# One copy instead of two for the projected rows of a graph attention layer, and a finish that adds the node's own row in two halves

## The chip, the cores and the metric

The kernel runs on one core of a Trainium2 chip. The metric is the device time of one execution in microseconds (us), as the median of several runs. Engines are TensorE (PE), VectorE (DVE), ScalarE (ACT), GpSimd (POOL) and the queues that issue DMAs (SP and POOL here).

## The reference

3125 nodes with 1024 features, 50000 edges sorted by target. A graph attention layer with 4 heads of 256 columns comes first and two graph layers with mean aggregation follow; each part has a residual.

```python
h = jnp.maximum(_layernorm(x), 0.0)
xp = (h @ W).reshape(N, H, C)                  # the projected rows
a_src = einsum('nhc,hc->nh', xp, att_src); a_dst = einsum('nhc,hc->nh', xp, att_dst)
e = leaky_relu(a_src[src] + a_dst[dst], 0.2)   # every node also has an edge to itself
alpha = softmax of e over the edges of each dst
out = segment_sum(xp[src] * alpha[:, :, None], dst)
x = x + relu(out + bias)
h = jnp.maximum(_layernorm(x), 0.0)
h1 = relu(h @ W_self0 + mean(h) @ W_neigh0 + b0)
x = x + (h1 @ W_self1 + mean(h1) @ W_neigh1 + b1)
```

## The kernel before

The nodes are cut into 25 tiles of 125 rows. Precision near float32 comes from pairs of float16 numbers: a high half and a low half that holds what the high one lost. A matrix product then takes three products of halves. The kernel runs in stages, one after the other, and between two stages all engines meet.

`normalize_x` (about 135 to 275 us) normalizes the input and projects the first 4 tiles beside it. `edge_scores` (to about 639 us) projects the other 21 tiles, in pieces between the small matmuls that fetch the scores of the edges, and turns the scores into weights. Both write each projected tile twice to DRAM. ACT takes the float32 sums out of PSUM into `rows` (L655, L1131) and copies them to float16 as the high half (L659, L1135). The low half is a subtraction, on DVE in the first stage (L705) and on POOL in the second (L1089). The POOL queue stores `rows` to `xp_rows` (L619, L1087) and the two halves to `xs_rows` (L621, L1091). `rows` is a single buffer: before ACT fills it again it waits for `xp_stored`, the store of the tile before, and in `edge_scores` also for `rows_lo`.

`aggregate` (to about 1333 us) gathers rows of `xs_rows` by the edges and sums them by target, weighted, into `acc`, which stays in SBUF. A node's edge to itself isn't in the list of edges.

`gat_finish` (1333 to 1657 us) adds that edge and does the rest of the layer. Its engines run over the tiles m side by side:

- SP loads x and `xp_rows` of tile m (L1621, L1622) into two slots each, once `x1_ready` says that tile m - 2 has been used, and stores the product of an older tile (L1627). After the loads of tile 1 it issues the load of 4 MB of split weights and that of b0, before the loads of tile 2.
- DVE does `values(m)`: 4 `scalar_tensor_tensor` instructions, one a head (L1682), for own row times own weight plus `acc`; 4 more (L1687) for the division and the bias; one for relu and residual (L1690); then the statistics (L1693 to L1697). Then `normalize(m)`: after ACT's square root, L1705 and L1706, the shift. Then `finish(m - 2)` (L1724), which takes the product of tile m - 2 out of PSUM, once `prod_done` is given. Between tiles 1 and 2 stands `bound` (L1714 to L1717 and three more).
- ACT writes the normalized row as float32 and as the high half (L1756, twice), and moves turned halves out of PSUM (L1742).
- POOL makes the low half (L1649, one `tensor_tensor`) and gives `lo_done`.
- PE works in the order: 16 of the 48 matmuls of tile n (L1787), the 16 transposes of tile n + 1 (L1775), which wait for `lo_done`, then the other 32 matmuls of tile n (L1791), after which it gives `prod_done`.

DVE's order within a tile and PE's are written out by hand and can't change with the times. Two aggregations, the second layer's products and the last product follow, to the end at 3406 us.

Of the kernel before, what the change touches and what calls it, by code (L numbers as in the profile page):

```python
# [11 lines left out]
def bass_gat_sage_sage(nc, x_in, src_in, dst_in, w_gat, att_src, att_dst, gat_bias,  # L12
# [63 lines left out]
    def scratch(name, shape, dt=f32):  # L76
        return nc.dram_tensor(name, shape, dt).ap()
# [2 lines left out]
    hn_rows = scratch("hn_rows", (N, 2 * D), f16)  # L80


    xp_rows = scratch("xp_rows", (N, D))
    xs_rows = scratch("xs_rows", (N, 2 * D), f16)
    slot_rows = scratch("slot_rows", (2, NS * CH), bf16)
    x1_rows = scratch("x1_rows", (N, D))
# [86 lines left out]
    with top:  # L173
# [354 lines left out]
        def normalize_x(w16, att_n, early_in):  # L528
            with ExitStack() as ctx:
# [26 lines left out]
                hn_ready, lo_done = sem("hn_ready"), sem("lo_done")  # L556
                turned, hi_moved, lo_moved, att_done, read_out = sem("turned"), sem("hi_moved"), sem("lo_moved"), sem("att_done"), sem("read_out")
                prod_done, rows_out, rows_hi, rows_lo = sem("prod_done"), sem("rows_out"), sem("rows_hi"), sem("rows_lo")
                xp_stored, xs_stored = sem("xp_stored"), sem("xs_stored")
                v_stats, v_norm = sem("v_stats"), sem("v_norm")  # L560
                block = ctx.enter_context(nc.Block())
                STEPS = NT + 2
# [49 lines left out]
                @block.gpsimd  # L612
                def _(g):
                    load_pieces = piece_loader(g, early_in)
                    for r in range(PIECE_BUFS):
                        load_pieces(r)
                    for p in range(FIRST):
                        g.wait_ge(rows_out, p + 1)
                        g.dma_start(tiles(xp_rows)[:, p:p + 1, :], rows[:, :].unsqueeze(1)).then_inc(xp_stored, 16)  # L619
                        g.wait_ge(rows_lo, p + 1)  # L620
                        g.dma_start(tiles(xs_rows)[:, p:p + 1, :], parts16[:, :].unsqueeze(1)).then_inc(xs_stored, 16)  # L621
                    g.wait_ge(xp_stored, 16 * FIRST)
                    g.wait_ge(xs_stored, 16 * FIRST)

                @block.scalar
                def _(a):
                    a.wait_ge(cleared, 1)
                    for s in range(STEPS):
                        if s < NT:
                            slot = s % 2  # L630
                            a.wait_ge(var_ready, s + 1)
                            a.activation(rstd[:, slot:slot + 1], mv[:, slot, 1:2], ACT.Sqrt).then_inc(std_ready, 1)
                            a.wait_ge(norm_ready, s + 1)
                            if s >= 2:
                                a.wait_ge(lo_done, s - 1)
                                a.wait_ge(turned, s - 1)
                                if stores_before(s):
                                    a.wait_ge(stored[slot], CUT * stores_before(s))
                            for dst in (hn[:, slot, :], a16[0:TN, slot, 0:D]):
                                last = a.activation(dst, x_sb[:, s % XS, :], ACT.Relu, bias=shift[:, slot:slot + 1],  # L640
                                                    scale=rstd[:, slot:slot + 1])
                            last.then_inc(hn_ready, 1)
                        if 2 <= s:
                            n = s - 2
                            a.wait_ge(turned, n + 1)
                            if n >= FIRST + 2:
                                a.wait_ge(att_done, n - 1)
                            a.activation(home(n)[:, 0], turn_ps[n % 2][:, 0], ACT.Copy).then_inc(hi_moved, 1)
                        piece = piece_of(s - 1)
                        if piece is not None and piece[1] == PIECES - 1:  # L650
                            p = piece[0]
                            a.wait_ge(prod_done, p + 1)
                            if p > 0:
                                a.wait_ge(xp_stored, 16 * p)
                            a.activation(rows[:, :], out_ps[0:TN, :], ACT.Copy, scale=1.0 / (UP * D)).then_inc(rows_out, 1)  # L655
                            a.wait_ge(rows_out, p + 1)
                            if p > 0:
                                a.wait_ge(xs_stored, 16 * p)
                            a.activation(parts16[:, 0:D], rows[:, :], ACT.Copy).then_inc(rows_hi, 1)  # L659
# [298 lines left out]
        def edge_scores(key_r, mask_r, att_n, w16, weight_e, high_e, early_in):  # L958


            with ExitStack() as ctx:
# [52 lines left out]
                now_ready = sem("now_ready")  # L1014
                spread, taken, kept = sem("spread"), sem("taken"), sem("kept")
                row_turned, row_moved, prod_done = sem("row_turned"), sem("row_moved"), sem("prod_done")
                rows_out, rows_hi, rows_lo, xp_stored, xs_stored = sem("rows_out"), sem("rows_hi"), sem("rows_lo"), sem("xp_stored"), sem("xs_stored")
                w_in = [sem(f"w_in{i}") for i in range(WBUF)]
                w_stored = [sem(f"w_stored{i}") for i in range(WBUF)]
                w_hi, w_lo, w_reduced, w_scaled = sem("w_hi"), sem("w_lo"), sem("w_reduced"), sem("w_scaled")  # L1020
# [60 lines left out]
                def _(g):  # L1081
                    load_pieces = piece_loader(g, early_in)

                    def low(p):
                        n = FIRST + p
                        g.wait_ge(rows_out, p + 1)
                        g.dma_start(tiles(xp_rows)[:, n:n + 1, :], rows[:, :].unsqueeze(1)).then_inc(xp_stored, 16)  # L1087
                        g.wait_ge(rows_hi, p + 1)
                        g.tensor_tensor(parts16[:, D:2 * D], rows[:, :], parts16[:, 0:D], ALU.subtract).then_inc(rows_lo, 1)  # L1089
                        g.wait_ge(rows_lo, p + 1)  # L1090
                        g.dma_start(tiles(xs_rows)[:, n:n + 1, :], parts16[:, :].unsqueeze(1)).then_inc(xs_stored, 16)  # L1091
# [10 lines left out]
                            low(p)  # L1102
                    for p in range(LEFT - AFTER, LEFT):
                        low(p)
                    g.wait_ge(xp_stored, 16 * LEFT)
                    g.wait_ge(xs_stored, 16 * LEFT)

                @block.scalar
                def _(a):
# [16 lines left out]
                    def evacuate(p):  # L1126
                        a.wait_ge(prod_done, p + 1)
                        if p > 0:
                            a.wait_ge(xp_stored, 16 * p)
                            a.wait_ge(rows_lo, p)  # L1130
                        a.activation(rows[:, :], out_ps[0:TN, :], ACT.Copy, scale=1.0 / (UP * D)).then_inc(rows_out, 1)  # L1131
                        a.wait_ge(rows_out, p + 1)
# [442 lines left out]
        def gat_finish(acc, acc_x, mem):  # L1575
            with ExitStack() as ctx:
                sb, ps, sem = opener(ctx, "fin")
                carve = carver(mem)
                x_sb = sb("x_sb", [TN, 2, D])
                xp_sb = carve([TN, 2, D])  # L1580
                a_t = [carve([P, 2, KT, P], f16) for _ in range(2)]
                b0_sb = carve([P, D])
                bias_sb = sb("bias_sb", [P, D])
# [32 lines left out]
                def _(sp):  # L1616
                    def load(m):
                        if m >= 2:
                            sp.wait_ge(x1_ready, m - 1)
                        for a, b in CUTS:  # L1620
                            sp.dma_start(x_sb[a:b, m % 2, :], x_in[m * TN + a:m * TN + b, :]).then_inc(x_loaded[m % 2], 16)  # L1621
                            sp.dma_start(xp_sb[a:b, m % 2, :], xp_rows[m * TN + a:m * TN + b, :]).then_inc(x_loaded[m % 2], 16)  # L1622

                    def store(n):
                        sp.wait_ge(read_out, n + 1)
# [31 lines left out]
                def _(v):  # L1657
# [11 lines left out]
                    v.wait_ge(bias_in, 16)  # L1669

                    def values(m):
                        PER = 2 + 1 + 3
                        slot = m % 2
                        step = chain(v, v_val, PER * m)
                        v.wait_ge(x_loaded[slot], 2 * CUT * (m // 2 + 1))
# [3 lines left out]

                        for h in range(H):  # L1680
                            cols = slice(h * C, (h + 1) * C)
                            last = v.scalar_tensor_tensor(val[:, slot, cols], xp_sb[:, slot, cols], own_n[:, m, h:h + 1],  # L1682
                                                          acc[:, m, cols], ALU.mult, ALU.add)
                        step(last)
                        for h in range(H):
                            cols = slice(h * C, (h + 1) * C)
# [364 lines left out]
```

## Time and profile before

| | |
|---|---|
| median of 3 runs | 3411.33 us (3408.95 to 3415.5) |
| profiled execution | 3407.41 us |
| its span, first to last instruction | 3405.8 us |
| mean granted clock of PE | 0.962 |
| PE busy | 2971.0 us, 87% |
| DVE busy | 2373.0 us, 70% |
| ACT busy | 1205.5 us, 35% |
| POOL busy | 1637.1 us, 48% |
| DMA | 934.91 MB, mean 275 GB/s |

Busy shares are means over stages with different limits. What an edit is worth has to be read in its own stage, from the waits of the engines there.

### The profile page before, as it was taken

How to read it: one execution, taken by the hardware profiler on the slowest of the kernel's cores; microseconds unless marked ns; L12 is line 12 of the kernel's file. 1: busy time of each engine (PE TensorE's matmuls, PEld its weight loads, DVE VectorE, ACT ScalarE, POOL GpSimd, SP SyncE). 2: the span in 40 equal slices, each digit the busy share in tenths (PEclk: the TensorE clock that was granted, in tenths of full speed). 3: DMA queues.
4: the chain of work that ended last, by engine and by line, in shares of the span. 5: the costliest groups of instructions: out<-in, count | busy, mean ns of one | idle time of the engine just before them, and what ended most of it. 6: DMA issues, size and time to landing. Idle time of an engine off the chain costs nothing. (4 is left out here: it accounts for less than half of the span.)

```text
span 3405.8 us, 66706 instructions
## 1 busy us (share of the span) xinstructions
PE 2971.0 (87%) x20462; PEld 1711.8 (50%) x20462; DVE 2373.0 (70%) x3944; ACT 1205.5 (35%) x2639; POOL 1637.1 (48%) x1592
## 2 busy tenths in 40 slices
PE   0477998399999996999799999998799999997998
PEld 0245665188888885444244444443344444443444
DVE  9687998699999998888466666664455555554333
ACT  3454443288888886444112222222000000001111
POOL 5102332267777774222466666662566666662000
PEclk9978999699999998999899999999899999998999
DMA  2797995388888888777699999995999999996444
GB/s 79 226 292 226 353 344 171 110 295 311 307 316 307 307 309 292 217 220 226 247 354 330 331 338 328 331 338 211 321 346 328 329 328 333 315 331 241 133 138 120
DMA packets 282530, 934.91 MB, mean 275 GB/s; under 512 B 53795, under 2 KB 54799, under 8 KB 282368
## 3 DMA queue, kind: packets, MB, share of 16 engines
q0 software_dynamic: 217792, 713.64, 59.9%
q1 hardware_dynamic: 64576, 219.26, 20.6%
q8 instruction: 83, 1.36, 0.2%
q14 instruction: 79, 0.65, 0.1%
HBM read 879.78 MB, written 130.57 MB: 297 GB/s over the span
## 5 line engine op out<-in xcount | busy, mean ns | idle before, releaser
L1522 PE MATMUL gagg_sum_ps<-gagg_got,gagg_hot_hi 128*128 128x256 f16 x3520 | 591.4, 273 | 92.8 <-ACT gagg_hot_hi L1493 58.8
L1493 ACT ACTIVATE gagg_hot_hi<-gagg_hot,all_mem 128x128 f16<-128x128 f16 x1760 | 538.0, 388 | 165.6 <-DVE gagg_hot L1433 165.4
L1410 POOL DMA_INDIRECT gagg_got<-xs_rows,all_idx x440 | 503.8, 1145 | 191.9 <-issue 131.4
L1410 POOL DMA_INDIRECT agg_got<-h_rows,all_idx x440 | 435.3, 989 | 317.8 <-PE agg_sum_ps L1538 175.9
L1838 POOL DMA_INDIRECT agg_got<-h_rows,all_idx x440 | 437.6, 994 | 268.2 <-PE agg_sum_ps L1991 145.7
L1458 DVE TENSOR_TENSOR sums_acc<-agg_sum_ps,sums_acc 125x1024 f32 x220 | 269.5, 1225 | 320.3 <-PE agg_sum_ps L1538 317.1
L1522 PE MATMUL gagg_sum_ps<-gagg_got,gagg_hot_lo 128*128 128x256 f16 x1760 | 481.5, 274 | 0.0
L1903 DVE TENSOR_TENSOR sums_acc<-agg_sum_ps,sums_acc 125x1024 f32 x220 | 268.9, 1222 | 246.9 <-PE agg_sum_ps L1991 245.0
L1991 PE MATMUL agg_sum_ps<-agg_got,all_mem 128*128 128x512 f16 x1760 | 415.4, 383 | 24.2 <-DVE all_mem L1872 16.7
L1538 PE MATMUL agg_sum_ps<-agg_got,agg_hot 128*128 128x512 f16 x1760 | 418.1, 381 | 17.1 <-DMA agg_got<-h_rows,all_idx 12.4
L1522 PEld LDWEIGHTS gagg_sum_ps<-gagg_got,gagg_hot_hi 128*128 128x128 f16 x3520 | 329.3, 98 | 136.3 <-ACT gagg_hot_hi L1493 68.2
L1439 DVE TENSOR_TENSOR gagg_hot_lo<-gagg_hot,all_mem 128x512 f16<-128x512 f16 x440 | 284.7, 689 | 9.3
L1991 PEld LDWEIGHTS agg_sum_ps<-agg_got,all_mem 128*128 128x128 bf16 x1760 | 170.7, 98 | 235.8 <-issue 29.9
L1976 PE MATMUL agg_out_ps<-agg_w,all_mem 128*128 128x512 f16 x1200 | 283.6, 381 | 2.0 <-ACT all_mem L1933 2.0
L1538 PEld LDWEIGHTS agg_sum_ps<-agg_got,agg_hot 128*128 128x128 bf16 x1760 | 167.4, 98 | 232.2 <-issue 36.6
L951 PE MATMUL agg_out_ps<-agg_w,all_mem 128*128 128x512 f16 x1200 | 283.5, 379 | 0.0
L1458 DVE TENSOR_TENSOR sums_acc<-gagg_sum_ps,sums_acc 125x1033 f32 x220 | 270.7, 1230 | 13.9 <-PE gagg_sum_ps L1527 12.0
L864 PE MATMUL neigh_out_ps<-neigh_w,neigh_a_t 128*128 128x512 f16 x1200 | 264.4, 381 | 4.7 <-DMA neigh_w<-split_w 4.7
L930 ACT ACTIVATE all_mem<-agg_turn_ps 128x2048 f16<-128x2048 f16 x25 | 46.9, 1877 | 601.2 <-PE agg_turn_ps L938 601.2
L1320 PE MATMUL edg_out_ps<-gatw_w,edg_a_t 128*128 128x512 f16 x1008 | 238.2, 381 | 5.3 <-ACT edg_rows L1131 5.3
L1925 ACT ACTIVATE all_mem<-sums_acc,all_deg_inv 125x1024 f16 x25 | 28.7, 1148 | 465.8 <-issue 402.1
L1976 PEld LDWEIGHTS agg_out_ps<-agg_w,all_mem 128*128 128x128 f16 x1200 | 117.6, 98 | 144.9 <-issue 2.4
(290 smaller groups left out, 4013.1 us busy)
## 6 DMA issues: line engine op xcount, KB each, us to landing
gatw_piece<-slot_rows POOLq DMA_DIRECT2D x56, 512.0 KB
split_w<-edg_w_out SPq DMA_DIRECT2D x32, 512.0 KB, 8.2
agg_got<-h_rows,all_idx POOLq DMA_INDIRECT x880, 7.0
x_rows<-fin_val POOLq DMA_DIRECT2D x25, 500.0 KB
h_rows<-fin_h POOLq DMA_DIRECT2D x25, 500.0 KB
out_dram<-neigh_rows POOLq DMA_DIRECT2D x25, 500.0 KB
norm_x_sb<-in_x_dram SPq DMA_DIRECT2D x25, 448.0 KB
fin_x_sb<-in_x_dram SPq DMA_DIRECT2D x25, 448.0 KB
```

The lines of the kernel that those rows point to most:

```text
L864: last = t.matmul(o, l, r, start=start, stop=stop)
L951: last = t.matmul(o, l, r, start=first, stop=final)
L1410: g.indirect_dma_start(out=got[:, k % R, :], out_offset=None, in_=rows_in[:, :], in_offset=bass.IndirectOffsetOnAxis(ap=idx[:, k:k + 1], a ...
L1439: v.tensor_tensor(hot_lo[:, u % HOTS, :, :], hot[:, u % HOTS:u % HOTS + 1, :].to_broadcast([P, H, P]), weight_e[:, ds(s, 1), 1, 0:H].rearr ...
L1458: v.tensor_tensor(acc[:, tl, 0:WIDE], sum_ps[n % 2][0:TN, 0:WIDE].rearrange("p (a d) -> p a d", a=1), acc[:, tl, 0:WIDE], ALU.add).then_in ...
L1493: last = a.activation(hot_hi[:, u % HOTS, h, :], hot[:, u % HOTS, :], ACT.Copy, scale=high_e[:, ds(s, 1), h])
L1522: t.matmul(sum_ps[n % 2][:, h * C:(h + 1) * C], hot_k[:, u % HOTS, h, :], got[:, u % R, part * D + h * C:part * D + (h + 1) * C], start=(u ...
L1538: last = t.matmul(sum_ps[n % 2][:, q * HALF:(q + 1) * HALF], hot[:, u % HOTS, :], got[:, u % R, cols], start=(u == steps[0] and part == 0) ...
L1838: g.indirect_dma_start(out=got[:, k % R, :], out_offset=None, in_=rows_in[:, :], in_offset=bass.IndirectOffsetOnAxis(ap=idx[:, k:k + 1], a ...
L1903: v.tensor_tensor(acc[:, ds(tile, 1), 0:D], sum_ps[g % 2][0:TN, :].rearrange("p (a d) -> p a d", a=1), acc[:, ds(tile, 1), 0:D], ALU.add). ...
L1976: last = t.matmul(o, l, r, start=start, stop=stop)
L1991: last = t.matmul(sum_ps[g % 2][:, q * HALF:(q + 1) * HALF], hot[:, u % R, :], got[:, u % R, cols], start=(u % PAIR == 0 and part == 0), s ...
```

## The change

The float32 copy is gone. `xs_rows`, the pair of halves, is the only copy. Its size per row is that of `xp_rows` (2048 float16 numbers instead of 1024 float32 ones, 4 KB each), so the finish loads as many bytes as before, in as many DMAs, into a tile of the same size. The finish adds the own row in two passes of 4 instructions: low half times weight plus `acc`, then high half times weight plus that result, with a semaphore step of its own between them. Where ACT waited for the float32 store before it refilled `rows`, it now waits for the low half's subtraction.

```diff
-    xp_rows = scratch("xp_rows", (N, D))
     xs_rows = scratch("xs_rows", (N, 2 * D), f16)
...
                     for p in range(FIRST):
                         g.wait_ge(rows_out, p + 1)
-                        g.dma_start(tiles(xp_rows)[:, p:p + 1, :], rows[:, :].unsqueeze(1)).then_inc(xp_stored, 16)
                         g.wait_ge(rows_lo, p + 1)
                         g.dma_start(tiles(xs_rows)[:, p:p + 1, :], parts16[:, :].unsqueeze(1)).then_inc(xs_stored, 16)
-                    g.wait_ge(xp_stored, 16 * FIRST)
...
                             if p > 0:
-                                a.wait_ge(xp_stored, 16 * p)
+                                a.wait_ge(rows_lo, p)
...
                     def low(p):
                         n = FIRST + p
                         g.wait_ge(rows_out, p + 1)
-                        g.dma_start(tiles(xp_rows)[:, n:n + 1, :], rows[:, :].unsqueeze(1)).then_inc(xp_stored, 16)
                         g.wait_ge(rows_hi, p + 1)
...
-                    g.wait_ge(xp_stored, 16 * LEFT)
...
                         if p > 0:
-                            a.wait_ge(xp_stored, 16 * p)
                             a.wait_ge(rows_lo, p)
...
-                xp_sb = carve([TN, 2, D])
+                xs_sb = carve([TN, 2, 2 * D], f16)
...
-                            sp.dma_start(xp_sb[a:b, m % 2, :], xp_rows[m * TN + a:m * TN + b, :]).then_inc(x_loaded[m % 2], 16)
+                            sp.dma_start(xs_sb[a:b, m % 2, :], xs_rows[m * TN + a:m * TN + b, :]).then_inc(x_loaded[m % 2], 16)
...
-                        PER = 2 + 1 + 3
+                        PER = 3 + 1 + 3
...
                         for h in range(H):
                             cols = slice(h * C, (h + 1) * C)
-                            last = v.scalar_tensor_tensor(val[:, slot, cols], xp_sb[:, slot, cols], own_n[:, m, h:h + 1],
+                            last = v.scalar_tensor_tensor(val[:, slot, cols], xs_sb[:, slot, D + h * C:D + (h + 1) * C], own_n[:, m, h:h + 1],
                                                           acc[:, m, cols], ALU.mult, ALU.add)
+                        step(last)
+                        for h in range(H):
+                            cols = slice(h * C, (h + 1) * C)
+                            last = v.scalar_tensor_tensor(val[:, slot, cols], xs_sb[:, slot, cols], own_n[:, m, h:h + 1],
+                                                          val[:, slot, cols], ALU.mult, ALU.add)
                         step(last)
```

## Rows read from the trace of the kernel before

**Rows 1.** Busy time by stretch: start:end, length, each engine, granted clock, DMA share

```profile
core 0: us, PE busy (x) PEld busy (x) DVE busy (x) ACT busy (x) POOL busy (x), PEclk, DMA share, GB/s
350.00:400.00 50.00, 48.88 (x548) 30.90 (x546) 49.25 (x78) 24.11 (x63) 16.88 (x21) 1.00 0.98 352
...
1354.00:1651.00 297.00, 287.02 (x1599) 139.50 (x1600) 226.44 (x385) 131.45 (x121) 79.89 (x74) 0.98 0.69 212
```

**Rows 2.** Timeline, DVE in one tile of the finish: start, duration, operation, [idle]

```profile
1453.56 0.21 DVE L1706 TENSOR_SCALAR fin_shift<-fin_mv,fin_rstd 125x1 f32<-125x1 f32 x1
...
1455.09 1.28 DVE L1724 SCALAR_TENSOR_TENSOR fin_rows<-fin_out_ps,fin_post,all_mem 125x1024 f32<-125x1024 f32 x1 [1.31 <-PE fin_out_ps L1791]
1456.29 3.63 DVE L1682 SCALAR_TENSOR_TENSOR fin_val<-all_mem,fin_own_n,sums_acc 125x256 f32<-125x256 f32 x4
1459.95 1.67 DVE L1687 SCALAR_TENSOR_TENSOR fin_val<-fin_val,fin_z,fin_bias_sb 125x256 f32<-125x256 f32 x4
...
1465.38 0.21 DVE L1706 TENSOR_SCALAR fin_shift<-fin_mv,fin_rstd 125x1 f32<-125x1 f32 x1
1466.51 1.28 DVE L1724 SCALAR_TENSOR_TENSOR fin_rows<-fin_out_ps,fin_post,all_mem 125x1024 f32<-125x1024 f32 x1 [0.92 <-PE fin_out_ps L1791]
```

**Rows 3.** Timeline, GpSimd and TensorE in the same tile and in an earlier one

```profile
1389.47 1.06 PE L1775 MATMUL fin_turn_ps<-all_ident,fin_h 128*128 128x128 f16 x16
...
1400.72 1.06 PE L1775 MATMUL fin_turn_ps<-all_ident,fin_h 128*128 128x128 f16 x16
...
1456.32 2.12 POOL L1649 TENSOR_TENSOR fin_h<-fin_h_sb,fin_h 125x1024 f16<-125x1024 f32 x1 [4.38 <-ACT fin_h L1756]
1458.50 1.07 PE L1775 MATMUL fin_turn_ps<-all_ident,fin_h 128*128 128x128 f16 x16
1459.40 7.07 PE L1791 MATMUL fin_out_ps<-fin_w,all_mem 128*128 128x512 f16 x32
...
1468.13 2.43 POOL L1649 TENSOR_TENSOR fin_h<-fin_h_sb,fin_h 125x1024 f16<-125x1024 f32 x1 [4.37 <-ACT fin_h L1756]
```

**Rows 4.** Timeline, DVE at the start of the finish, and its last tile

```profile
1360.76 1.22 DVE L1714 TENSOR_REDUCE fin_largest<-all_mem 128x1 f32<-128x1024 f32 x1 [1.87 <-DMA all_mem<-in_L_gnn_b_dram]
...
1365.80 1.68 DVE L1682 SCALAR_TENSOR_TENSOR fin_val<-all_mem,fin_own_n,sums_acc 125x256 f32<-125x256 f32 x4 [1.29 <-DMA all_mem<-xp_rows]
...
1372.94 0.21 DVE L1706 TENSOR_SCALAR fin_shift<-fin_mv,fin_rstd 125x1 f32<-125x1 f32 x1
1373.31 1.28 DVE L1724 SCALAR_TENSOR_TENSOR fin_rows<-fin_out_ps,fin_post,all_mem 125x1024 f32<-125x1024 f32 x1
...
1383.38 0.21 DVE L1706 TENSOR_SCALAR fin_shift<-fin_mv,fin_rstd 125x1 f32<-125x1 f32 x1
1386.22 1.28 DVE L1724 SCALAR_TENSOR_TENSOR fin_rows<-fin_out_ps,fin_post,all_mem 125x1024 f32<-125x1024 f32 x1 [2.63 <-PE fin_out_ps L1791]
...
1395.21 0.21 DVE L1706 TENSOR_SCALAR fin_shift<-fin_mv,fin_rstd 125x1 f32<-125x1 f32 x1
...
1628.08 0.21 DVE L1706 TENSOR_SCALAR fin_shift<-fin_mv,fin_rstd 125x1 f32<-125x1 f32 x1
```

**Rows 5.** Groups by line, whole kernel: busy and mean, then idle before

```profile
L1211 DVE SCALAR_TENSOR_TENSOR edg_w_out<-edg_w_buf,all_w_up,edg_w_out 128x1024 f16<-128x1024 f32 x32 | 44.6, 1394 | 1.9 <-ACT edg_w_out L1142 1.9
L1690 DVE SCALAR_TENSOR_TENSOR fin_val<-fin_val,fin_x_sb 125x1024 f32<-125x1024 f32 x25 | 30.6, 1225 | 0.9
```

**Rows 6.** Who waited for whom, 300 to 560 us: us, times, longest

```profile
ACT edg_w_out L1142 <- DMA edg_w_buf<-in_L_gnn_W_neigh_dram: 7.2, 3, 3.3
DVE edg_mask L1189 <- DMA gatw_piece<-slot_rows: 3.6, 1, 3.6
ACT edg_w_out L1142 <- DMA edg_w_buf<-in_L_gnn_W_self_dram: 2.9, 2, 1.6
```

**Rows 7.** Busy time by stretch, two stretches with gaps on TensorE

```profile
140.00:160.00 20.00, 15.74 (x175) 9.29 (x173) 18.18 (x33) 11.56 (x14) 0.00 (x0) 0.74 0.87 262
1374.00:1384.00 10.00, 7.68 (x48) 3.84 (x47) 8.84 (x16) 4.96 (x6) 3.51 (x3) 1.00 0.80 235
```

## The prediction on record

> **What bounds the kernel now.** I read first the busy time by stretch, for the stages that the diff touches, then the timeline of the finish tile by tile, then the waits of `edge_scores`.
>
> In the finish PE looks like the bound: busy 287.02 of 297 us [rows 1]. Two transposes without a wait between them stand 11.25 us apart, 1389.47 and 1400.72 [rows 3], and this is PE's own work for one tile. But the shifts (L1706) of tiles 4 and 24 stand at 1395.21 and 1628.08 [rows 4], 20 tiles apart, which is 11.64 us a tile. So PE isn't quite the bound. The timeline shows what is: a ring through all engines that takes two tiles for one turn. From the shift of one tile (1453.56) it is 2.76 us to POOL's subtraction (1456.32); 2.18 to the transposes (1458.50); 8.01 to DVE's L1724 (1466.51), since 32 matmuls of 7.1 us end just before; 1.20 from there to the next L1682 (as 1455.09 to 1456.29); and 9.09 from L1682 to the shift after it (1456.29 to 1465.38) [rows 2, 3]. The sum is 23.24 us for two tiles, 11.62 for one, beside 11.64 measured. That is the check that the ring is the bound, with DVE's `values` as one of its legs.
>
> DVE's own order is shorter. L1724 can follow the shift after 0.37 us (1372.94 to 1373.31 [rows 4]), so it needs 0.37 + 1.20 + 9.09 = 10.66 us a tile; the rest, about 1 us, is its wait for PE, 1.31 and 0.92 us in the two tiles shown [rows 2].
>
> The 9.09 us hold a stall. Four instructions of L1682 take 1.68 us alone [rows 4], but 3.63 us when POOL's subtraction starts 0.03 us after them [rows 2, 3]: 1.95 us lost, nearly POOL's 2.12. So while POOL's subtraction runs, L1682 stands still. A new instruction of this kind can be held up in the same way, but the hold lasts only as long as POOL's one instruction, so the second pass moves it and adds no second one.
>
> **The change part by part.**
>
> New work on DVE: 4 instructions a tile, in a leg of the ring. The low pass is L1682 with another first operand. The trace has no such instruction with a float16 operand beside float32 ones on 256 columns, so I bound it. L1211 mixes both types, on 1024 columns, and takes 1394 ns in the mean; L1690, all float32 on 1024 columns, takes 1225 [rows 5]. So float16 buys nothing there. I take the price of L1682: 1.68 us for four and 0.03 us to the next pass (1456.29 + 3.63 to 1459.95 [rows 2]), 1.71 us a tile. The lower bound is two columns in the time of one: L1690's 1225 ns for 1024 columns and 420 for 256 give 1.05 ns a column, so half the columns of four instructions would save 4 x 128 x 1.05 = 0.54 us and leave 1.2. The upper bound is the price stretched as L1211 is against L1690, 1394/1225, 1.9.
>
> The Trainium skill (VectorE: DVE Perf Modes, the section on the TRN2 errata) prices such an instruction at 58 cycles and its columns, 327 ns for 256 at 0.96 GHz. The row has 1.68 us for four, 420 ns each [rows 4], so the trace does not agree, and by the page's figure the new pass would be an estimated 1.3 us and the whole sum some 5 us smaller.
>
> The ring's new length: 23.24 + 1.71 = 24.95 for two tiles, 12.47 a tile. One more effect: with DVE's wait nearly gone, L1682 starts about 0.9 us before POOL's subtraction, not beside it. When DVE is ahead, POOL waits for the instruction under way and takes 2.43 instead of 2.12 us (1468.13 [rows 3]). With all of these 0.31 us it is 12.63. I take 12.55, 0.91 over 11.64. DVE alone would need 10.66 + 1.71 = 12.37, and PE 11.25: both are shorter, so the ring stays the bound. Twenty tiles (4 to 24) give 20 x 0.91 = 18.2 us.
>
> The start is walked by the shifts [rows 4]. Two tiles of `values` come before `bound`: 3.4 us of new work. `bound` waits 1.87 us for b0, and L1682 of tile 2 waits 1.29 us for its load. Both loads are queued behind the 4 MB of weights, and I leave them where they are. The two waits take up 3.16 of the 3.4. But POOL's subtraction of tile 1, 3.4 us later too, now reaches into L1682 of tile 2 (1.68, so not held, before) and costs about 0.7. So the shift of tile 2 comes 0.3 + 1.7 + 0.7 = 2.7 us late, at 1375.6. Tile 3 follows on DVE alone, + 1.7: 4.4 late, at 1387.8. Tile 4 is held by the ring: 1375.6 + 2.76 + 2.5 + 8.01 = 1388.9 for L1724, + 1.20 + 9.09 + 1.71 - 0.1 = 1400.8 for its shift, 5.6 late (the wait of 2.63 us before L1724 at 1386.22 is what shrinks). The last tiles are PE's and hide nothing, for `values(24)` is the last that the transposes wait for. The finish: 5.6 + 18.2 = 23.8 us longer.
>
> Removed in `edge_scores` and `normalize_x`: 25 stores of 500 KB and their issue, about 0.5 us of POOL each. In `edge_scores` the DMA engines are 98% busy at 352 GB/s while PE is busy 48.88 of 50 us [rows 1]. If DMA set the pace, 16 stores between 300 and 560 us would be worth 16 x 1.45 = 23 us. The waits for DMA there sum to 13.7 us [rows 6], 10.1 of them ACT's for weights that are only split beside the main work, and PE has few gaps. I take 0.5 us, between 0 and 6. POOL's issue stood before its wait for ACT's high half and was hidden by that. The wait that takes the place of `xp_stored`, `rows_lo`, was there already in `edge_scores`, and `normalize_x` evacuates four tiles in its 140 us, so the subtraction is long done when ACT asks for it. The last tile's `xs_rows` store, which ends the stage, is issued after POOL's subtraction, not after the other store.
>
> The loads of the finish keep their count, bytes and queue. SP issues the load for tile m + 2 when `x1_ready` comes, 1.71 us later in its tile; it has nearly two tiles to land. Nothing else waits for it. ACT and POOL shift with the ring.
>
> Sum against the profiled execution: 3407.4 + 23.8 - 0.5 = 3430.7 us. It lies 3.9 under the median of the runs (3411.3), so the same difference of 23.3 on the median is 3434.6, and I predict 3435.
>
> **The rivals.** (a) The ring gives way and DVE's order alone sets the pace, because some leg through POOL or PE is shorter than read: 12.37 - 11.64 = 0.73 a tile, 14.6 + 5.6 = 20: 3431. The sum of the legs speaks against it.
> (b) A cheap float16 pass, 1.2 us: the ring 23.24 + 1.2 + 0.3 = 24.74, 12.37 a tile, 0.73 over before, 14.6 and about 3.5 at the start: 3429. L1211 against L1690 speaks against it [rows 5].
> (c) Nothing is shared between tiles and each pays the full pass: 25 x 1.71 = 43: 3454. The ring's turn of two tiles speaks against it, and so do the two DMA waits at the start.
> (d) The clock. PE's gaps grow from 0.4 to 1.3 us a tile. In 140 to 160 us, with PE busy 15.74 of 20, the granted clock is 0.74 [rows 7], so in part 1.2 GHz instead of 2.4. At 0.8 PE's tile would be 11.25/0.8 = 14.1 us, 2.4 over 11.64, 20 times: with the start 3466. Against it: in 1374 to 1384, with a gap of 2.3 us and PE busy 7.68 of 10, the clock is 1.00 [rows 7].
> (e) Faster: `edge_scores` runs at the pace of its DMAs, and stores away are time back. It decides from 24 us, and 25 stores of 1.45 us are worth 36; all of them would have to sit on the path, 3411 - 12 = 3399. PE's 98% there and 13.7 us of waits cap it well below.
> (f) No change to be told from none, 3411: DVE's work hidden in its wait. Its wait is about 1 us and the pass 1.7, so only if (b) and (e) come together.
>
> **How the numbers follow.** The ring 0.64, (a) 0.12, (b) 0.10, (c) 0.04, (d) 0.04, (e) 0.03, (f) 0.03. The predicted time is the ring's. Its own range is 3430 to 3440: 12.47 to 12.63 a tile is 3 us, the relief in `edge_scores` and the runs' spread the rest. The range of 8 in 10 takes in (a) and (b), with up to 6 us of relief, and upwards half the way to (c): 3423 to 3446. A measurement of this kernel tells 0.2%, 7 us, from no change. Faster is (e), 0.03; same is (f), 0.03; slower is the rest, 0.94.
>
> **What the profile after would show.** Two groups of 100 instructions where L1682 was, each about 1.7 us for four when not held, and one hold a tile of 1.9 us, in the first pass. Shifts 12.5 to 12.6 us apart. DVE's wait for PE before L1724 down from about 1 us to 0.3. PE's wait for POOL before the transposes in every tile, about 1.3 us, clock 1.00. The finish 24 us longer and `edge_scores` as long as before within 2 us. I am wrong if shifts stand 12.4 apart without a wait of DVE (a), if the new pass is short (b), if the clock falls in the finish (d), or if `edge_scores` ends much earlier (e).

## The result, and the profile after

The kernel before took 3410.69 us as the median of 6 runs (3406.05 to 3415.5), the changed kernel 3426.09 us (3421.82 to 3430.14). The ratio is 1.0041, with a 95% interval of 1.0028 to 1.0054: slower by 9.6 to 18.4 us. Predicted were 3435 and a range of 3423 to 3446. The sign and the mechanism in the finish hold; the size of the whole came out a third smaller. The profiled executions differ alike, 3421.82 against 3407.41 us.

The head of the page of the kernel after, and what its DMAs moved:

```profile
span 3420.2 us, 66804 instructions
PE 2971.5 (87%) x20462; PEld 1710.8 (50%) x20462; DVE 2424.2 (71%) x4044; ACT 1205.2 (35%) x2639; POOL 1613.6 (47%) x1567
...
DMA packets 278931, 922.11 MB, mean 270 GB/s; under 512 B 53320, under 2 KB 54324, under 8 KB 278768
```

DVE does 51 us more, PE as much as before, and the DMAs move 12.8 MB less (934.91 before), which is the 25 stores. A DVE that is busy 51 us longer, its stalls included, in a kernel 15 us slower says that much of it found room or was paid for elsewhere.

**One tile of the finish.** The DVE timeline of the kernel after; L1676 is the new low pass, L1681 the high pass, L1705 the shift, L1723 the finish of an older tile:

```profile
1426.65 0.21 DVE L1705 TENSOR_SCALAR fin_shift<-fin_mv,fin_rstd 125x1 f32<-125x1 f32 x1
1427.27 1.28 DVE L1723 SCALAR_TENSOR_TENSOR fin_rows<-fin_out_ps,fin_post,all_mem 125x1024 f32<-125x1024 f32 x1 [0.40 <-PE fin_out_ps L1790]
1428.47 3.53 DVE L1676 SCALAR_TENSOR_TENSOR fin_val<-all_mem,fin_own_n,sums_acc 125x256 f32<-125x256 f16 x4
1432.03 1.67 DVE L1681 SCALAR_TENSOR_TENSOR fin_val<-all_mem,fin_own_n,fin_val 125x256 f32<-125x256 f16 x4
1433.74 1.67 DVE L1686 SCALAR_TENSOR_TENSOR fin_val<-fin_val,fin_z,fin_bias_sb 125x256 f32<-125x256 f32 x4
...
1439.17 0.21 DVE L1705 TENSOR_SCALAR fin_shift<-fin_mv,fin_rstd 125x1 f32<-125x1 f32 x1
1439.79 1.28 DVE L1723 SCALAR_TENSOR_TENSOR fin_rows<-fin_out_ps,fin_post,all_mem 125x1024 f32<-125x1024 f32 x1 [0.40 <-PE fin_out_ps L1790]
1440.99 1.27 DVE L1676 SCALAR_TENSOR_TENSOR fin_val<-all_mem,fin_own_n,sums_acc 125x256 f32<-125x256 f16 x3
```

POOL and PE in the same tile:

```profile
1429.41 2.31 POOL L1643 TENSOR_TENSOR fin_h<-fin_h_sb,fin_h 125x1024 f16<-125x1024 f32 x1 [4.38 <-ACT fin_h L1755]
1431.77 1.07 PE L1774 MATMUL fin_turn_ps<-all_ident,fin_h 128*128 128x128 f16 x16 [1.09 <-POOL fin_h L1643]
1432.68 7.07 PE L1790 MATMUL fin_out_ps<-fin_w,all_mem 128*128 128x512 f16 x32
```

Walk the ring. From the shift at 1426.65 it is 2.76 us to POOL, 2.36 to the transposes, 8.02 to DVE's L1723 at 1439.79, 1.20 to the next L1676, and 10.70 from an L1676 to its shift (1428.47 to 1439.17). That is 25.04 us, 12.52 a tile, and the shifts stand 12.52 apart. Against [rows 2, 3] one leg grew by 1.61 (the new pass) and one by 0.18 (POOL waits for the DVE instruction under way). PE now waits 1.09 us for POOL in each tile, where before it waited 0.3 or 0.7 us in about half of them; DVE's wait for PE, mostly between 0.92 and 1.72 us before, has shrunk to 0.40. The first pass is held while POOL runs: 3.53 instead of 1.67. The second, with the same float16 operand, takes 1.67.

**The start and the end of the finish**, DVE after, beside [rows 4]:

```profile
1330.64 1.67 DVE L1676 SCALAR_TENSOR_TENSOR fin_val<-all_mem,fin_own_n,sums_acc 125x256 f32<-125x256 f16 x4 [3.48 <-DMA fin_bias_sb<-in_L_gnn_bias_dram]
...
1350.93 1.22 DVE L1713 TENSOR_REDUCE fin_largest<-all_mem 128x1 f32<-128x1024 f32 x1 [0.15 <-DVE fin_shift L1705]
1352.18 0.16 DVE L1714 TENSOR_TENSOR fin_spread<-all_w_down 128x1 f32<-128x1 f32 x1
...
1354.72 2.19 DVE L1676 SCALAR_TENSOR_TENSOR fin_val<-all_mem,fin_own_n,sums_acc 125x256 f32<-125x256 f16 x4 [1.43 <-DMA all_mem<-xs_rows]
...
1364.09 0.21 DVE L1705 TENSOR_SCALAR fin_shift<-fin_mv,fin_rstd 125x1 f32<-125x1 f32 x1
...
1376.23 0.21 DVE L1705 TENSOR_SCALAR fin_shift<-fin_mv,fin_rstd 125x1 f32<-125x1 f32 x1
...
1389.27 0.21 DVE L1705 TENSOR_SCALAR fin_shift<-fin_mv,fin_rstd 125x1 f32<-125x1 f32 x1
...
1639.49 0.21 DVE L1705 TENSOR_SCALAR fin_shift<-fin_mv,fin_rstd 125x1 f32<-125x1 f32 x1
```

The last two are the shifts of tiles 4 and 24: 250.22/20 = 12.51 us a tile.

**The stages.** I took the first and last start of the instructions that open and close each stage. In us; `pause` runs from the last evacuation of `edge_scores` to the first matmul of the weighted aggregation, `finish` from the first L1682 or L1676 to the last L1724 or L1723:

| | before | after | difference |
|---|---|---|---|
| first edge matrix, start | 281.9 | 280.5 | -1.4 |
| `edge_scores` | 338.6 | 337.2 | -1.4 |
| pause | 30.1 | 28.4 | -1.7 |
| weighted aggregation | 679.2 | 673.0 | -6.2 |
| to the first own row | 12.4 | 11.5 | -0.9 |
| finish | 309.4 | 332.2 | +22.8 |
| first mean aggregation | 680.7 | 680.5 | -0.2 |
| second mean aggregation | 686.8 | 690.8 | +4.0 |
| the other stretches | | | -0.6 |

So the finish lost 22.8 us, as the ring says, and everything before it gave back 11.6, where I had 0.5; what follows the finish took 3.2 back. (The second mean aggregation has the same code in all kernels. In two profiles of the kernel before it took 686.8 and 692.6 us, so 4 us is within its scatter.)

### The profile page after: what moved, and what is told of

Same layout as the page of the kernel before. It is cut to its first block and busy times, and to the rows that moved or that the text cites. A ratio compares the mean times of both kernels' runs of the same rounds, so it can differ in the third digit from the quotient of the medians.

```text
span 3420.2 us, 66804 instructions
## 1 busy us (share of the span) xinstructions
PE 2971.5 (87%) x20462; PEld 1710.8 (50%) x20462; DVE 2424.2 (71%) x4044; ACT 1205.2 (35%) x2639; POOL 1613.6 (47%) x1567
## 5 line engine op out<-in xcount | busy, mean ns | idle before, releaser
L1404 POOL DMA_INDIRECT gagg_got<-xs_rows,all_idx x440 | 491.0, 1116 | 196.4 <-issue 138.5
L1990 PE MATMUL agg_sum_ps<-agg_got,all_mem 128*128 128x512 f16 x1760 | 415.3, 383 | 24.1 <-DVE all_mem L1871 16.7
L1452 DVE TENSOR_TENSOR sums_acc<-gagg_sum_ps,sums_acc 125x1033 f32 x220 | 270.8, 1231 | 11.6 <-PE gagg_sum_ps L1521 9.0
```

Source lines behind the costliest of these rows:

```text
L1404: g.indirect_dma_start(out=got[:, k % R, :], out_offset=None, in_=rows_in[:, :], in_offset=bass.IndirectOffsetOnAxis(ap=idx[:, k:k + 1], a ...
L1452: v.tensor_tensor(acc[:, tl, 0:WIDE], sum_ps[n % 2][0:TN, 0:WIDE].rearrange("p (a d) -> p a d", a=1), acc[:, tl, 0:WIDE], ALU.add).then_in ...
L1990: last = t.matmul(sum_ps[g % 2][:, q * HALF:(q + 1) * HALF], hot[:, u % R, :], got[:, u % R, cols], start=(u % PAIR == 0 and part == 0), s ...
```

## The experiments

They ran on at least three chips, of two speeds. `thin`, `before_again`, `reorder` and `dve_low` ran on a chip of speed A, as did, by its times, the pair above; there the kernel before takes 3410.7 to 3414.6 us. The others ran on two chips of speed B, where it takes 3535.5 and 3536.6. Each ratio is against the kernel before on the same chip; where a difference of whole kernels is given in us, it is of the medians.

### The two halves of the change, alone

`fin_only` is the kernel before with the finish of the kernel after: all stores, and the two passes (the last two parts of the change's diff). `after_again` is the kernel after once more, on this chip.

> Both stores are kept, with their waits and the place of every tensor in DRAM; only the finish is changed (it loads the halves and adds them in two passes). If the finish costs what the ring of two tiles says, it is 22 to 24 us longer than before's and the whole kernel is 22 to 24 us slower than before, 7 us slower than the full change. If the whole is only 15 us slower, the finish is cheaper in the time of the runs than in the one profile, and the stores give nothing back.

`stores_only` is the kernel after with one pass, so it leaves out the low half of the node's own row:

```diff
                         for h in range(H):
                             cols = slice(h * C, (h + 1) * C)
-                            last = v.scalar_tensor_tensor(val[:, slot, cols], xs_sb[:, slot, D + h * C:D + (h + 1) * C], own_n[:, m, h:h + 1],
-                                                          acc[:, m, cols], ALU.mult, ALU.add)
-                        step(last)
...
                             last = v.scalar_tensor_tensor(val[:, slot, cols], xs_sb[:, slot, cols], own_n[:, m, h:h + 1],
-                                                          val[:, slot, cols], ALU.mult, ALU.add)
+                                                          acc[:, m, cols], ALU.mult, ALU.add)
```

> The float32 stores are gone, and the finish has one pass as before; it leaves out the low half of the node's own row. If the stores give back what is missing, this is 5 to 11 us faster than before, with the finish as long as before's (11.6 us a tile). If the missing time is scatter of the one profile, it is within 3 us of before.

> The changed kernel again. The ring theory expects the same 12.52 us a tile in the finish to 0.02 us. If the aggregations before and after the finish are scatter, their lengths differ from the first profile by several us; if they are an effect of the change, the first aggregation is again 6 us shorter than before's and the last 4 us longer.

Measured at speed B, on one chip: `fin_only` 3558.26 us, ratio 1.0061 (1.0044 to 1.0078), +23 us; `stores_only` 3528.44, 0.9979 (0.9968 to 0.9991), -7 us; the kernel after 3547.81, 1.0028 (1.0013 to 1.0043), +12 us. The finish took 332.7, 308.6 and 332.7 us. All three load the halves, so the loss of 24.1 us in the finish is the second pass and not the load. The stores' removal is a gain of its own: 7 us by `stores_only`, with an interval of 3 to 11, and 10.5 by the kernel after against `fin_only`, whose single runs overlap.

### Bytes, issue, or the tensor itself

`thin` is `fin_only` with each float32 store cut to 16 of its 125 rows. Issue, semaphore and waits stay, and 87% of the bytes go:

```diff
-                        g.dma_start(tiles(xp_rows)[:, n:n + 1, :], rows[:, :].unsqueeze(1)).then_inc(xp_stored, 16)
+                        g.dma_start(tiles(xp_rows)[0:16, n:n + 1, :], rows[0:16, :].unsqueeze(1)).then_inc(xp_stored, 16)
```

> The finish of the change, with all 25 issues of the float32 store, its semaphore and its waits as before, but each stores 16 of 125 rows, 13% of the bytes. If it is the bytes on the DMA engines that cost time, this is 13 to 16 us slower than before, like the full change, with 255 to 258 us of rounds. If it is POOL's issue or the wait for the store, it is 21 to 23 us slower. If the longer pause behind edge_scores belongs to the semaphore or the issue, it stays 30 us; if to the bytes, it is 28.4.

> The kernel before again, on the chip of this group, for its stages. If the float32 stores cost time in the rounds of edge_scores, the time from the first to the last use of the fetched scores is 259 to 266 us here and 255 to 258 us in the kernel below that stores little. If that was scatter, they are alike. The pause from the last tile's evacuation to the first matmul of the aggregation is 30.1 us if it belongs to the stores.

`layout` is the kernel after with the float32 tensor still allotted in its old place and one row of it written, so that `xs_rows` and all behind it lie where they lay:

```diff
+    xp_rows = scratch("xp_rows", (N, D))
     xs_rows = scratch("xs_rows", (N, 2 * D), f16)
...
+                    sp.dma_start(xp_rows[0:1, :], x_in[0:1, :]).then_inc(touched, 16)
```

> The full change, but the old float32 tensor stays in its place in DRAM and gets one row of 4 KB, so that all later tensors lie where they lay before. If the shorter aggregation of the layer comes from the new place of the rows that it gathers, it is 6 us longer here than in the full change and the kernel 21 us slower than before. If it comes from the stores or from scatter, the kernel is 15 us slower than before, as the full change.

> The full change with the old tensor left in its place in DRAM, on this chip. Profiles of the quicker chip gave the aggregation 679.2, 677.6 and 679.4 us with that tensor there and 673.0, 674.1 and 674.8 without it. If the place of the gathered rows does this, it is 677 to 680 us here and the kernel 5 us slower than the full change; if it is scatter or comes with the stores, it is 673 to 675.

Measured: at speed A `thin` took 3429.68 us, 1.0041 (1.0026 to 1.0057), 15 us slower than before and within the 13 to 16 expected if it is the bytes; a second profile of the kernel before took 3410.4. At speed B `layout` took 3555.33, 1.0055 (1.0042 to 1.0068), and on the other chip 3548.62, 1.0033 (1.0022 to 1.0044). The first is 20 us slower than before, near the 21 expected if the place matters, the second 12, near the 15 expected if it doesn't; the stages below decide.

The windows view of 300 to 500 us, in the middle of `edge_scores`, shows what the bytes do; the columns are those of [rows 1]. The kernel before:

```profile
300.00:500.00 200.00, 193.20 (x2147) 122.43 (x2144) 181.46 (x305) 95.32 (x231) 63.48 (x78) 1.00 0.94 330
```

The kernel after:

```profile
300.00:500.00 200.00, 196.87 (x2196) 125.29 (x2195) 182.51 (x311) 99.30 (x236) 60.19 (x67) 1.00 0.90 308
```

`thin`:

```profile
300.00:500.00 200.00, 196.60 (x2197) 125.27 (x2195) 181.94 (x311) 100.67 (x242) 68.41 (x82) 1.00 0.92 314
```

PE does 3.7 us more work (193.20 against 196.87) in the same 200, with the DMA engines at 0.90 instead of 0.94. `thin`, which keeps the issues and the waits, has it too. The other three profiles with full stores have 189.20, 191.13 and 192.59 us of PE there, and the ten without them, `thin` among them, 196.27 to 198.09. So it is the bytes, or the packets that carry them, which `thin` cuts alike. From the first to the last round of edges it is 258.8, 260.6, 262.8 and 266.1 us in the four profiles with full stores, 262.1 in the mean, and 253.5 to 257.9 in the ten others, `thin` among them, 255.6 in the mean. The bytes cost some 6.5 us.

The pause behaves otherwise: 30.1 or 30.2 us in all five profiles with the float32 store, `thin` among them, 28.3 or 28.4 in all nine without it, `layout` among them. These 1.8 us go with the store's issue or its semaphore, not with its bytes nor with the tensor.

The weighted aggregation took 677.6, 679.2 and 679.4 us at speed A in the three profiles with the float32 tensor and 673.0, 674.1 and 674.8 in the three without: some 5 us for a stage whose code is the same. At speed B there is no such step (771.8 to 774.2 in eight profiles of both kinds). `layout` was to tell whether the place of the tensors is the cause, and it ran at speed B both times, where it makes no difference to this stage. So these 5 us are measured, and their cause stays open.

### Opening the ring

If the ring is the bound, DVE's own order (12.37 us a tile) should appear once DVE does the own-row passes of the next tile before it waits for PE's product. `reorder` does that with the kernel after:

```diff
                     for m in range(NT + 2):
                         if m < NT:
                             values(m)
                             normalize(m)
+                        if m + 1 < NT:
+                            own(m + 1)
                         if m == 1:
                             bound()
                         if m >= 2:
                             finish(m - 2)
```

> The full change, but DVE makes both passes of the next tile before it takes the product of the tile before out of PSUM. Same instructions, another order. If the ring of two tiles bounds the finish, it falls open: 13.26 us from a shift to the product, 1.20 and 5.43 to the next shift but one, 19.9 for two tiles, and DVE alone sets 12.3 us a tile, 0.2 less than 12.52: about 5 us faster than the full change, and PE's wait no longer moves. If DVE's order had been the bound all along, nothing changes.

`dve_low` is `reorder`, with DVE in POOL's place for the low half of the normalized row:

```diff
-                        g.tensor_tensor(h16[0:TN, slot, D:2 * D], h_sb[:, :], h16[0:TN, slot, 0:D], ALU.subtract).then_inc(lo_done, 1)
...
+                        v.tensor_tensor(h16[0:TN, slot, D:2 * D], h_sb[:, :], h16[0:TN, slot, 0:D], ALU.subtract).then_inc(lo_done, 1)
```

> As the reordered one, and the low half of the normalized row is made by DVE (1.25 us) instead of POOL (2.1 us), between the passes and the product. If POOL's subtraction holds DVE up for 1.9 us a tile, DVE now needs 0.37 + 3.42 + 1.25 + 1.20 + 5.43 = 11.67 us a tile, the finish is 20 us shorter than in the full change and the kernel 3 to 8 us faster than before. If the hold were something else, DVE would need 13.5 us a tile and it would be 20 us slower than the full change.

Measured at speed A: `reorder` 3470.1 us, 1.0173 (1.0155 to 1.019), and `dve_low` 3525.49, 1.0336 (1.0316 to 1.0356). Both went far the other way: `reorder` was expected 5 us faster than the kernel after, `dve_low` 3 to 8 us faster than the kernel before. The DVE timeline of `reorder` says why:

```profile
1479.93 0.21 DVE L1712 TENSOR_SCALAR fin_shift<-fin_mv,fin_rstd 125x1 f32<-125x1 f32 x1
1484.01 2.27 DVE L1678 SCALAR_TENSOR_TENSOR fin_val<-all_mem,fin_own_n,sums_acc 125x256 f32<-125x256 f16 x4 [3.87 <-DMA all_mem<-xs_rows]
...
1494.64 0.21 DVE L1712 TENSOR_SCALAR fin_shift<-fin_mv,fin_rstd 125x1 f32<-125x1 f32 x1
```

And its SP queue:

```profile
1474.62 0.76 SPq L1621 DMA_DIRECT2D part_rows<-fin_rows  x2
...
1476.41 0.45 SPq L1616 DMA_DIRECT2D all_mem<-xs_rows  x1
...
1477.58 0.36 SPq L1616 DMA_DIRECT2D all_mem<-xs_rows  x1
```

The loads of a tile stand on SP behind the store of an older product (the `part_rows` line), and that store waits for DVE's finish. Once the passes come before that finish, the load is late, here by 3.87 us and in most tiles by 3 or more, and a tile takes 14.71. In `dve_low` DVE waits 5.0 to 6.8 us for the same load, and a tile takes 17.4 in the mean of 20. So neither says anything yet of the ring. `dve_low` does say what the hold is: with no subtraction on POOL, both passes take 1.67 or 1.68 us in all 25 tiles.

`reorder_lag` mends that: SP stores the product one tile later (`LAG = 4` for 3), so the loads go out ahead of it, and `bound` comes before the passes of tile 2.

```diff
-                LAG = 3
+                LAG = 4
...
                         if m == 1:
                             bound()
+                        if m + 1 < NT:
+                            own(m + 1)
                         if m >= 2:
```

> The reordered finish again, with SP's store of a product moved one tile back (LAG 4 for 3), so that the load of the next tile no longer stands behind it, and bound ahead of the passes of tile 2. The reordered kernel waited 3 to 4 us a tile for its load. Without that wait the ring theory expects DVE alone to set 12.3 us a tile, the finish 4 to 6 us shorter than the full change's 332, and no wait for DMA. If a load is still late, the tile stays above 12.6 us.

It took 3543.37 us at speed B, 1.0018 (1.0007 to 1.003). DVE in `reorder_lag`:

```profile
1714.15 0.21 DVE L1712 TENSOR_SCALAR fin_shift<-fin_mv,fin_rstd 125x1 f32<-125x1 f32 x1
1714.62 1.68 DVE L1678 SCALAR_TENSOR_TENSOR fin_val<-all_mem,fin_own_n,sums_acc 125x256 f32<-125x256 f16 x4 [0.25 <-DVE fin_shift L1712]
1716.33 3.54 DVE L1683 SCALAR_TENSOR_TENSOR fin_val<-all_mem,fin_own_n,fin_val 125x256 f32<-125x256 f16 x4
...
1726.53 0.21 DVE L1712 TENSOR_SCALAR fin_shift<-fin_mv,fin_rstd 125x1 f32<-125x1 f32 x1
```

The shifts stand 12.38 apart, from the fourth tile to the last but two no wait for PE or a load is left, and the finish takes 329.3 us instead of 332.7, 3.4 us less where 4 to 6 were expected. The ring is open, DVE alone is the bound at the 12.37 that I had worked out for it, and the ring had been worth 0.14 us a tile. The hold sits in the second pass now, still once a tile.

### A better version

`merge_lag` adds the two halves in one instruction of 1024 columns and weights the sum in four, gives DVE the low half, and keeps `LAG = 4`:

```diff
-                            last = v.scalar_tensor_tensor(val[:, slot, cols], xs_sb[:, slot, D + h * C:D + (h + 1) * C], own_n[:, m, h:h + 1],
-                                                          acc[:, m, cols], ALU.mult, ALU.add)
+                        step(v.tensor_tensor(val[:, slot, :], xs_sb[:, slot, 0:D], xs_sb[:, slot, D:2 * D], ALU.add))
+                        for h in range(H):
+                            cols = slice(h * C, (h + 1) * C)
+                            last = v.scalar_tensor_tensor(val[:, slot, cols], val[:, slot, cols], own_n[:, m, h:h + 1],
+                                                          acc[:, m, cols], ALU.mult, ALU.add)
```

> The full change with everything that the findings point to: order and loads as in the kernel above, the two halves first added in one instruction of 1024 columns (1.27 us) and then weighted in 4, and the low half of the normalized row on DVE, not POOL. Theory of the hold: DVE needs 0.37 + 1.27 + 1.71 + 1.25 + 1.20 + 5.43 = 11.23 us, PE 11.25, so 11.3 us a tile, the finish about 302 us against 309 before, and the kernel 10 to 18 us faster than before. If POOL's subtraction did not hold DVE, it would be 1.9 us a tile slower than that and no faster than before.

`before_lag` gives the kernel before the same order, `LAG = 4` and the low half on DVE, with its single pass and all its stores.

> The kernel before, with the same order, loads and low half on DVE, and its float32 copy and single pass kept. DVE needs 10.6 us a tile, PE 11.25: about 11.3, the finish some 302 us and the kernel 6 to 9 us faster than before. The difference to the merged kernel is what the removed stores are worth alone, 6 to 10 us, if the finish is PE's in both.

On one chip of speed B `merge_lag` took 3521.68 us, 0.9958 (0.9942 to 0.9973), and `before_lag` 3526.16, 0.9977 (0.9963 to 0.9991): 15.0 and 10.5 us faster than before. So the order and the low half on DVE bring 10.5 us without the change (6 to 9 were expected). DVE in `merge_lag`:

```profile
1565.19 0.21 DVE L1706 TENSOR_SCALAR fin_shift<-fin_mv,fin_rstd 125x1 f32<-125x1 f32 x1
1565.65 1.23 DVE L1674 TENSOR_TENSOR fin_val<-all_mem 125x1024 f32<-125x1024 f16 x1 [0.25 <-DVE fin_shift L1706]
1566.91 1.67 DVE L1677 SCALAR_TENSOR_TENSOR fin_val<-fin_val,fin_own_n,sums_acc 125x256 f32<-125x256 f32 x4
1568.62 1.23 DVE L1713 TENSOR_TENSOR fin_h<-fin_h_sb,fin_h 125x1024 f16<-125x1024 f32 x1
...
1576.38 0.21 DVE L1706 TENSOR_SCALAR fin_shift<-fin_mv,fin_rstd 125x1 f32<-125x1 f32 x1
```

PE in the same kernel:

```profile
1571.42 1.06 PE L1786 MATMUL fin_turn_ps<-all_ident,fin_h 128*128 128x128 f16 x16
...
1582.68 1.06 PE L1786 MATMUL fin_turn_ps<-all_ident,fin_h 128*128 128x128 f16 x16
```

The low half costs DVE 1.23 us, and the hold that it takes away had cost 1.86. What the merged pass brings by itself no run shows. A tile is 11.19 us on DVE, with no wait but the 0.25 in it, and 11.26 on PE, whose transposes wait for nothing after tile 1: PE is the bound at last. The finish takes 305.3 us, less than with one pass and the old order (308.6 in `stores_only`). `before_lag` has 300.1 us there, 5.2 less, and still is the slower kernel, by 4.5 us of the medians (the single runs overlap, and 4.5 is less than the 6 to 10 expected, because its finish is the shorter one). So its stores cost it some 9.7 us, a median and a profile taken together. In the two profiles 5.1 of them lie before the finish and 3.6 in the two mean aggregations, whose code is the same.

## Why the prediction was right, and where it was off

**The ring: right.** 24.95 us plus POOL's lengthening gave 12.55 a tile; 12.51 was measured over 20 tiles, and the finish grew by 22.8 where 23.8 was forecast. `fin_only` shows it alone: its finish takes 332.7 us, against 308.6 with one pass on the same chip (`stores_only`). `reorder_lag` opens the ring and gets 12.38, the pace that rival (a) gave for a ring that doesn't bind. The ring lies only 0.14 us a tile above DVE's own order, so the two are told apart by the wait of 0.40 us that DVE still has for PE, and by `reorder_lag`.

**The price of the pass: right.** 1.67 us for four instructions with a float16 operand, L1681, against 1.67 with float32 ones, L1686. Rival (b) is out. The hold stayed one a tile, from tile 4 on in the first pass, as argued. The Trainium skill (VectorE: DVE Perf Modes, the errata section) also states, for a float32 `tensor_tensor`, columns + 151 cycles at 0.96 GHz: 424 ns for 256, an estimated 1.70 us for four. The rows' 1.67 us and 0.03 to the next pass agree with that, and not with the 58 cycles that I had weighed.

**The start: right in size, partly for a wrong reason.** Counted from the first own-row pass (1342.16 before, 1330.64 after), the shifts of tiles 2, 3 and 4 came 2.7, 4.4 and 5.6 us later, the three figures forecast. But I had both waits absorb 3.16 us. The wait for b0 went (1.87 to 0.15), the one for the load of tile 2 did not (1.29 to 1.43). What went in its place was a hold that I had not looked at: one instruction of `bound` on 128x1, L1715, had taken 1.55 us beside POOL's subtraction in the kernel before, and takes 0.16 now (L1714). The rows of the kernel before:

```profile
1342.16 1.67 DVE L1682 SCALAR_TENSOR_TENSOR fin_val<-all_mem,fin_own_n,sums_acc 125x256 f32<-125x256 f32 x4 [4.26 <-DMA fin_bias_sb<-in_L_gnn_bias_dram]
...
1361.43 2.12 POOL L1649 TENSOR_TENSOR fin_h<-fin_h_sb,fin_h 125x1024 f16<-125x1024 f32 x1 [4.37 <-ACT fin_h L1756]
...
1362.01 1.55 DVE L1715 TENSOR_TENSOR fin_spread<-all_w_down 128x1 f32<-128x1 f32 x1
```

**The clock: right.** Granted 1.00 in 1500 to 1550 and in 1600 to 1650 us, with PE's gaps of 1.09 us, and 0.98 over 1354 to 1675 as over 1354 to 1651 before [rows 1]; rival (d) is out. Rival (c), 43 us, is out.

**The stores: mis-sized.** The term that failed is "I take 0.5 us, between 0 and 6" for the relief in `edge_scores`. By the medians the relief was 7.1 us (`stores_only`) and 10.5 (`fin_only` against the kernel after); with the finish of the profiles taken off it was 9.7 (`before_lag` against `merge_lag`) and 22.8 - 15.4 = 7.4 in the pair itself. Over all profiles two terms explain about 8.3 of it: 6.5 us for the bytes in `edge_scores` and 1.8 for the pause. The profiled pair splits otherwise: 1.4 us in `edge_scores` (so "as long as before within 2 us" held there), 1.4 ahead of it, 1.7 in the pause, 7.1 from there to the finish, and 3.2 the other way behind it, 8.4 in all. The kernel before was quick in this profile, 338.6 us in `edge_scores`, where its second profile has 341.9. So the size is well supported, and its split in a single pair isn't. The error of method: I took the listed waits for DMA as the cap on what DMA can cost [rows 6]. In a stage with the DMA engines at 0.98 [rows 1] what bytes cost need not stand in the list under DMA: that list has only the waits which end on a transfer directly. That the rest shows as other engines' waits further on is argued, not shown. 23.8 - 0.5 should have read about 23.8 - 8.5 = 15.3, beside the 14.4 of the profiles and the 15.4 of the medians. It was a part of rival (e), at a quarter of its 36 us.

**A wrong sentence that cost nothing here.** I wrote that the load of the finish "has nearly two tiles to land". It has less than one: in the kernel after, SP issues it from 1430.37 for the pass at 1440.99, after the store of an older product. That was enough for this change, and it was what broke `reorder` and `dve_low`.

**Open:** which of issue and semaphore costs the 1.8 us of the pause; why the weighted aggregation was 5 us shorter at speed A in the kernels without the float32 tensor. Whether it is where the tensors lie wasn't tried at that speed.

## What to carry to other kernels

An instruction that is added to a ring which spans two tiles costs half its time per tile as long as the ring binds (here 1.71 us gave 0.87 a tile), so the ring is to be summed and the sum held against the measured period before anything is priced. Bytes taken from a stage whose DMA engines were 0.94 busy were worth some 6.5 us here, though few waits named a DMA: price such bytes by a trial with thin transfers, not by the list of waits. Before an instruction is moved up in an engine's order, look at what the queue that loads its operand stands behind.

## What the runs showed of the hardware

**One kernel, chips of two speeds, 3.6% apart.** Three quarters of it are in the weighted aggregation, whose rows are gathered by indirect DMAs. The windows view of 700 to 1200 us, columns as above, of the kernel before at speed A:

```profile
700.00:1200.00 500.00, 469.34 (x4718) 418.00 (x4716) 484.27 (x843) 411.97 (x1348) 387.13 (x337) 1.00 0.89 311
```

`before_lag`, which differs only in the finish, at speed B:

```profile
700.00:1200.00 500.00, 419.99 (x4130) 370.23 (x4129) 423.90 (x739) 359.87 (x1178) 339.39 (x296) 1.00 0.82 275
```

The same code moves 275 GB/s instead of 311 and issues 296 gathers instead of 337, at the same granted clock. The stage takes 773 us there and 679 here, the mean aggregations some 2% more (680 and 691 against 692 and 707). No run tells why. So runs on different chips can't be compared in microseconds.

**The hold by GpSimd has nearly one size.** Four DVE instructions with two SBUF inputs lost 1.86 to 1.96 us in all to a POOL subtraction of 2.12 to 2.45 us that started beside them or early within them, wherever they stood: the first pass (3.53, and 3.63 in [rows 2]), the second pass (3.54 in `reorder_lag`) or the division (3.54 in tile 1 of the kernel before). They lost less, 1.55 us, in four tiles of the kernel before, and 0.52 in tile 2 of the kernel after, where the subtraction had begun 0.37 and 1.40 us before them. POOL in its turn takes 2.26 to 2.45 us instead of 2.12 when a DVE instruction is under way. The held instruction of 128x1 above ended at 1363.56, as the subtraction did at 1363.55. The Trainium skill (SBUF — State Buffer, the section on the two sides of SBUF) calls this an exclusive lock of a shared port pair, held for the whole instruction, and these rows agree.
